# A fused two-pass attention layer, one core: three queues put in another order inside one unit of work

## What is computed

```
q, k, v = xn @ Wq * scale, xn @ Wk, xn @ Wv          # 16 heads of 64
attn    = softmax(causal(q @ k.T))                   # 1024 x 1024 a head
out     = attn @ v
adj     = clip(attn + eye, 0, 1);  deg = adj.sum(-1)
feats   = v
for l in 0, 1:                                       # two graph layers
    h     = feats @ gnn_w[l] + gnn_b[l]
    feats = gelu(adj @ h / deg + feats)
out     = out + feats @ lin_w + lin_b
return layernorm(concat(out) @ Wo)
```

## Time and profile before

| | |
|---|---|
| median of 3 runs | 1946.68 us (1943.61 to 1954.76) |
| the profiled execution's own time | 1947.65 us |
| its span, first to last instruction | 1945.8 us |
| busy in the span: PE, DVE, ACT, POOL | 74%, 60%, 45%, 43% |
| first attention | about 30 to 1044 us |
| busy in it: PE, DVE, ACT, POOL | 850, 547, 555, 522 us |
| granted PE clock in it, share of full speed | 0.96 |
| granted PE clock over the span | 0.874 |
| one whole unit, 312.33 to 372.73 us | 60.40 us, of which PE busy 51.69 |

### The profile page before, as it was taken

The page is one execution under the profiler, slowest core; times in us unless marked ns, Lnnn a source line. Parts: engine busy times, 40 slices in busy tenths (PEclk is TensorE's granted clock), DMA queues, the critical chain, the costliest instruction groups (busy, mean ns, idle before and its releaser), DMA issues. The chain is left out here.

```text
span 1945.8 us, 26818 instructions
## 1 busy us (share of the span) xinstructions
PE 1446.5 (74%) x8265; PEld 935.1 (48%) x8265; DVE 1175.9 (60%) x2921; ACT 881.4 (45%) x1838; POOL 834.7 (43%) x564
## 2 busy tenths in 40 slices
PE   3788888889878888888885877975328575667776
PEld 2555555555555555555544545653325321222466
DVE  4556555565546555565555854467672479999844
ACT  2456555565545555565643622322102175545334
POOL 1455445564444445665551010000005207999535
PEclk9899999999999999999998866887558777989868
DMA  1000000000000000000000000000521212322112
GB/s 54 6 6 1 5 5 5 5 0 5 6 6 1 7 6 5 5 0 5 0 1 13 1 7 6 12 20 0 186 33 37 71 35 84 102 77 92 57 45 84
DMA packets 42464, 53.45 MB, mean 27 GB/s; under 512 B 8529, under 2 KB 29930, under 8 KB 42130
## 3 DMA queue, kind: packets, MB, share of 16 engines
q1 hardware_dynamic: 39634, 46.84, 7.9%
q0 software_dynamic: 2752, 5.65, 1.2%
HBM read 42.82 MB, written 9.26 MB: 27 GB/s over the span
## 5 line engine op out<-in xcount | busy, mean ns | idle before, releaser
L372 POOL TENSOR_TENSOR l0a_A<-l0a_A,l0a_share 128x256 f32<-128x256 f32 (+7 forms) x128 | 269.6, 2107 | 147.3 <-DVE l0a_share L929 147.0
L489 ACT ACTIVATE l0a_A<-l0a_ring,l0a_low 128x512 f32<-128x512 f32 (+3 forms) x384 | 217.6, 577 | 116.1 <-DVE l0a_low L922 74.9
L688 PE MATMUL l0a_tr<-main_ident,l0a_A 128*128 128x128 f32 x1152 | 174.3, 289 | 39.0 <-DVE l0a_E L934 22.7
L934 DVE COPY l0a_E<-l0a_tr 128x512 f32<-128x512 f32 (+1 forms) x160 | 102.0, 638 | 157.8 <-PE l0a_tr L688 157.8
L919 DVE TENSOR_REDUCE l0a_low_part<-l0a_ring 128x2 f32<-128x1024 f32 (+3 forms) x128 | 130.5, 1021 | 97.5 <-PE l0a_ring L669 90.9
L688 PEld LDWEIGHTS l0a_tr<-main_ident,l0a_A 128*128 128x128 f32 x1152 | 136.5, 148 | 79.3 <-issue 57.3
L2857 PE MATMUL mx_ysum<-mx_hst,main_ident 128*128 128x512 f32 x256 | 134.1, 658 | 41.5 <-POOL mx_hst L2976 33.7
L2991 POOL TENSOR_TENSOR mx_dBu<-mx_XI,mx_BB 128x1024 f32<-128x1024 f32 x64 | 139.5, 2207 | 50.0 <-DVE mx_DT L3031 50.0
L378 POOL TENSOR_TENSOR l0a_T<-l0a_VW,l0a_small 128x512 f32<-128x512 f32 x32 | 33.4, 1043 | 277.2 <-DVE l0a_small L952 277.2
L697 PE MATMUL l0a_agg<-l0a_E,l0a_F 128*64 128x512 f32 (+3 forms) x768 | 143.9, 504 | 2.6 <-ACT l0a_U L510 2.6
L697 PE MATMUL l0a_agg<-l0a_E,l0a_VH 128*64 128x512 f32 (+3 forms) x768 | 130.9, 489 | 13.3 <-ACT l0a_E L495 13.3
(11 more groups left out here) (507 smaller groups left out, 3519.6 us busy)
## 6 DMA issues: line engine op xcount, KB each, us to landing
mx_BB<-mx_brows SPq DMA_DIRECT2D x32, 512.0 KB, 3.6
l0a_wp<-in_wqkv SPq DMA_DIRECT2D x16, 192.0 KB
moe_rows<-moe_XR SPq DMA_DIRECT2D x2, 1032.0 KB
moe_Wg<-in_f_wg SPq DMA_DIRECT2D x8, 256.0 KB, 5.7
moe_Wu<-in_f_wu SPq DMA_DIRECT2D x8, 256.0 KB, 5.9
moe_Wd<-in_f_wd SPq DMA_DIRECT2D x8, 256.0 KB, 6.0
moe_Y<-rt_zeros SPq DMA_DIRECT2D x2, 1024.0 KB, 10.9
e_back<-moe_Y SPq DMA_DIRECT2D x8, 256.0 KB, 5.1
```

What stands on the lines that cost most here:

```text
L372: pool.tensor_tensor(a, a, spread(share[:, it, :], [P, 2, w]), ALU.mult).then_inc(shared, 1)
L489: act.activation(A[:, it % 3, h, c0:c0 + n], pair(k % 2)[:, h, 0:n], ACT.Exp, bias=low[:, it, h:h + 1], accum_out=s).then_inc(exp_done, 1)
L688: mm = pe.transpose(tr[n % 2][:, at:at + P], A[:, it % 3, h, t * P:(t + 1) * P], ident[:, :])
L934: dve.tensor_copy(dst, src).then_inc(turned_dve, 1)
```

## The change

Everything keeps its instructions and their shapes; they stand in another order, and the weights of one unit that is never computed are loaded and split too.

- **Weights.** `weights_hi(u + 1)` and `weights_lo(u + 1)` now stand inside the scores of body g, one body earlier than before: ACT does it ahead of the last two exponentials' pieces, POOL between `shares(u, 6)` and `out2(g, 0)`. SP loads one more set.
- **Late score pieces.** On PE `mix` moves from behind pieces 3 and 5 to behind pieces 7 and 9, the tiles of `second(g, 1)` are spread further, and both `product2` come behind pieces 10 and 11. ACT, DVE and POOL move the steps that hang on them. POOL's `out_sum` stand ahead of `shares(u, 5)` and `shares(u, 6)`, and `out2(g, 0)` ahead of `shares(u, 7)`.
- **Turn 11** moves from the end of the scores behind `attend(g, 0)`. Its copy on DVE now stands behind `own_share(g, 0)` and `own_factors(g, 0)`, which come from behind the copies of turns 13 to 19 to the head of the body.
- **Body.** `values(u, 0)` stands ahead of `attend(g, 1)`; `set_own(g, 1)` behind the first two maxima of the scores.

The diff, without that one function of PE:

```diff
--- before.py
+++ after.py
@@ -343,8 +343,7 @@
                 with sp.Fori(0, PAIRS - 1) as i:
                     g = i + b * PAIRS if b else i
                     weights(bass.ds((i + 1) * P, P), g + 1)
-                if b < NB - 1:
-                    weights(slice(0, P), PAIRS * (b + 1))
+                weights(slice(0, P), PAIRS * (b + 1))
 
         @block.gpsimd
         def _(pool):
@@ -412,13 +411,13 @@
                         weights_lo(0)
                 keep_vb(0, 0)
                 keep_vb(0, 1)
-                for it in range(ST):
+                for it in range(ST - 1):
                     shares(0, it)
+                weights_lo(1)
+                shares(0, ST - 1)
 
             def body(g, prev, nb):
                 u, more, third = g + 1, nb is not None, prev is not None
-                if more:
-                    weights_lo(u)
                 own_part(g, 0)
                 own_part(g, 1)
                 if more:
@@ -432,19 +431,20 @@
                     shares(u, 3)
                     keep_vb(u, 0)
                     keep_vb(u, 1)
+                    shares(u, 4)
                 if third:
                     out_sum(g, prev, 0)
                 if more:
-                    shares(u, 4)
+                    shares(u, 5)
                 if third:
                     out_sum(g, prev, 1)
+                if more:
+                    shares(u, 6)
+                    weights_lo(u + 1)
                 out2(g, 0)
                 if more:
-                    shares(u, 5)
+                    shares(u, 7)
                 out2(g, 1)
-                if more:
-                    shares(u, 6)
-                    shares(u, 7)
 
             def tail(n, at):
                 out_sum(n, at, 0)
@@ -537,29 +537,29 @@
                 if more:
                     exps(u, 2)
                     exps(u, 3)
-                if third:
-                    keep_gl(g, 0)
-                if more:
                     turn_out(u, 0)
                     exps(u, 4)
                     exps(u, 5)
-                if third:
-                    keep_gl(g, 1)
-                if more:
                     turn_out(u, 2)
                     exps(u, 6)
                     exps(u, 7)
+                if third:
+                    keep_gl(g, 0)
+                if more:
                     turn_out(u, 4)
-                if second:
-                    keep_u2(g, 1)
-                if more:
                     turn_out(u, 6)
                     exps(u, 8)
                     exps(u, 9)
+                if second:
+                    keep_u2(g, 1)
+                if third:
+                    keep_gl(g, 1)
+                if more:
                     turn_out(u, 8)
-                    turn_out(u, 10)
+                    weights_hi(u + 1)
                     exps(u, 10)
                     exps(u, 11)
+                    turn_out(u, 10)
                 if second:
                     keep_ua(g)
 
@@ -580,7 +580,6 @@
             def body(g, prev, nb):
                 u, more, third = g + 1, nb is not None, prev is not None
                 if more:
-                    weights_hi(u)
                     keep_comp(u)
                 keep_ut(g, 0)
                 if more:
@@ -600,9 +599,10 @@
                     keep_v(u, 0)
                 if third:
                     keep_ft(g, 0)
+                if more:
+                    keep_v(u, 1)
+                if third:
                     keep_ft(g, 1)
-                if more:
-                    keep_v(u, 1)
                 gelu1(g, 1)
                 scores(u if more else None, g, prev)
 
@@ -776,39 +776,44 @@
...
@@ -827,6 +832,7 @@
                     pe.wait_ge(turned_act, g * NK + 6)
                     composite(u)
                 attend(g, 0)
+                turn(g, 11)
                 if more:
                     pe.wait_ge(exp_done, g * NEXP + (NEXP - 2))
                     if not third:
@@ -838,15 +844,16 @@
                 if more:
                     pe.wait_ge(exp_done, (g + 1) * NEXP)
                     project(u, ring[1], 1, nb, k_ready)
-                turn(g, 14, 15)
+                turn(g, 14, 15, 16, 17)
                 product1(g, 0)
-                turn(g, 16, 17, 18, 19)
+                turn(g, 18, 19)
+                if more:
+                    values(u, nb, 0)
                 attend(g, 1)
-                if more:
-                    values(u, nb, 0)
+                if third:
+                    turn_f(g, 0)
                 product1(g, 1)
                 if third:
-                    turn_f(g, 0)
                     turn_f(g, 1)
                 if more:
                     values(u, nb, 1)
@@ -865,7 +872,7 @@
                 more = n < NB * PAIRS
                 pe.wait_ge(exp_done, (n + 1 if more else n) * NEXP)
                 pe.wait_ge(turned_act, n * NK + 6 if more else n * NK)
-                pe.wait_ge(turned_dve, n * NK + 6 if more else n * NK)
+                pe.wait_ge(turned_dve, n * NK + 5 if more else n * NK)
                 pe.wait_ge(ot_kept, n * 2 - 2)
                 out_tiles(0, PAIRS - 1, 0, 1)
                 turn_f(n, 0)
@@ -977,6 +984,9 @@
                 more, second = u is not None, g is not None
                 if more:
                     row_low(u, 0, 1)
+                if second:
+                    set_own(g, 1)
+                if more:
                     row_share(u, 0)
                     row_low(u, 2)
                     row_share(u, 1)
@@ -991,22 +1001,20 @@
                     row_share(u, 4)
                     row_low(u, 7)
                     turn_out(u, 5)
-                if second:
-                    out2(g, 0)
-                if more:
                     row_low(u, 8)
                     row_share(u, 5)
                     row_low(u, 9)
                     turn_out(u, 7)
-                if second:
-                    out2(g, 1)
-                if more:
                     row_low(u, 10)
                     row_share(u, 6)
                     row_low(u, 11)
+                if second:
+                    out2(g, 0)
+                if more:
                     turn_out(u, 9)
-                    turn_out(u, 11)
                     row_share(u, 7)
+                if second:
+                    out2(g, 1)
 
             def first():
                 composite_lo(0)
@@ -1018,6 +1026,9 @@
                 u, more = g + 1, nb is not None
                 if more:
                     composite_lo(u)
+                own_share(g, 0)
+                own_factors(g, 0)
+                turn_out(g, 11)
                 turn_out(g, 13)
                 if more:
                     keep_q_lo(u)
@@ -1026,14 +1037,11 @@
                     keep_k_lo(u)
                 turn_out(g, 17)
                 turn_out(g, 19)
-                own_share(g, 0)
-                own_factors(g, 0)
+                own_share(g, 1)
+                own_factors(g, 1)
                 out1(g, 0)
                 set_own(g, 0)
-                own_share(g, 1)
-                own_factors(g, 1)
                 out1(g, 1)
-                set_own(g, 1)
                 scores(u if more else None, g)
 
             def tail(n, prev):
```

More of the change, by code:

```diff
@@ L778, in scores @@
                     score(u, 2, 3)
+                    turn(u, 0, 1, prev=prev)
+                if two:
+                    second(g, 1, 0, 1)
+                if more:
+                    score(u, 4, 5)
+                    turn(u, 2, 3)
+                if two:
+                    second(g, 1, 2, 3, 4)
+                if more:
+                    score(u, 6)
+                if two:
+                    second(g, 1, 5)
+                if more:
+                    score(u, 7)
                 if three:
@@ L782, in scores @@
                 if more:
-                    turn(u, 0, 1, prev=prev)
+                    turn(u, 4, 5)
                 if two:
-                    second(g, 1, 0)
+                    second(g, 1, 6)
                 if more:
-                    score(u, 4, 5)
+                    score(u, 8, 9)
+                if two:
+                    second(g, 1, 7)
+                if more:
+                    turn(u, 6)
                 if three:
@@ L790, in scores @@
                 if more:
-                    turn(u, 2, 3)
+                    turn(u, 7, 8)
+                    score(u, 10, 11)
                 if two:
-                    second(g, 1, 1, 2, 3)
-                if more:
-                    score(u, 6)
-                if two:
-                    second(g, 1, 4)
-                if more:
-                    score(u, 7)
-                    turn(u, 4, 5)
-                if two:
-                    second(g, 1, 5, 6, 7)
                     product2(g, prev, 0)
                 if more:
-                    score(u, 8, 9)
-                    turn(u, 6, 7, 8)
+                    turn(u, 9, 10)
```

(3 more changed lines are left out.)

24 lines of the change are left out of this document (12 added, 12 removed).

## The result

| | before | after |
|---|---|---|
| median of 11 runs each | 1946.68 us (1940.12 to 1954.76) | 1959.4 us (1955.79 to 1964.05) |
| ratio, 95% interval | | 1.0063 (1.0046 to 1.0080) |
| profiled execution, its span | 1947.65, 1945.8 us | 1956.93, 1955.2 us |
| busy in the span: PE, DVE, ACT, POOL | 74%, 60%, 45%, 43% | 74%, 65%, 45%, 43% |
| first instruction of the layer behind the attention | 1063.3 us | 1074.2 us |

The changed kernel is 0.6% slower. I had forecast 1967 us, 1.0% slower, for the reason that the records now show: a wait taken out at one place came back at another. The size was too large: attention ends 10.9 us later where I had forecast 20.5.

What follows compares the result with a forecast made beforehand. PE's queue with its waits was taken to set the 60.40 us unit. Seven units at +1.1 and six at +1.8 (+18.5), batch starts 0 and -3, last unit +5: +20.5 on 1947.65, so 1968, median 1967 us; range 1938 to 1990.

Steps and rivals of the forecast that it cites:

- piece 0 to 4: Score pieces 0 to 4 on PE: 10.20 us instead of 9.76, with turn 1 waiting about 1.0 for POOL.
- T to composite: From score piece 10's start (T) to the composite on PE: 7.30 us instead of 5.22, waiting for ACT's copy of turn 10.
- composite to Q: From the composite to the Q projection on PE: 3.27 us instead of 6.52, with no pause for POOL's weights.
- Q to piece 0, with the clock: Q projection to the next unit's score piece 0 on PE: 24.2 us at full clock plus 1.3 for slowed clock; before 21.93.
- Q to turn 13: Q's start to turn 13's start on PE: 6.2 us, as POOL's scaling holds DVE's diagonal ahead of turn 11's copy.
- no hold: Rival: DVE and POOL don't hold each other; turn 13 starts 1.9 behind Q, unit 55.6, 1888 us; chance 0.13.
- early diagonal: Rival: DVE's diagonal is issued before POOL's long scaling; 2 to 3 us a unit less, about 1930 us; chance 0.07.
- Turn 13 to piece 0: PE from turn 13 to the next unit's score piece 0: 17.5 us plus the turn's 0.49, at full clock.
- The clock: Behind PE's 4.3 us pause before turn 13, slowed work costs 1.3 us a unit, bounds 0 and 2.4.
- The batches' ends: A batch's first body has no `out_sum`: about 0 in batch one, -3 in batch two, where POOL has nothing left.
- The last unit: No weights to wait for; it pays the late turn 13 in full, some 8 us, less gains and swallowed waits: +5.
- the clock rival: Rival: the clock stays up or its loss is hidden; 59.9 a unit, +4 in all, 1950 us; chance 0.17.

Runs made afterwards that it cites:

- experiment 1: The changed kernel with DVE's diagonal and its factors moved behind the copies of turns 11 and 13: 1953.19 us, ratio 0.9890 to the kernel before.
- experiment 2: The changed kernel with each diagonal instruction replaced by a one-input row sum (TENSOR_REDUCE), so other factors: 1952.62 us, ratio 0.9874 to the kernel before.
- experiment 7: The kernel before with only the first half's diagonal and factors moved to the head of DVE's body: 1975.94 us, ratio 0.9992.
- experiment 8: The changed kernel with one-input row sums for the diagonal and the copies of turns 11 and 13 ahead of the factors: 1918.24 us, ratio 0.9695.
- experiment 3: The kernel before with only the weights split one unit further ahead: 1903.07 us, ratio 0.9631.
- experiment 5: The kernel before with weights a unit ahead, turn 11 behind the first aggregation and the next values ahead of the second: 1888.74 us, ratio 0.9545.

## Why the prediction was right, and where its size was off

The steps by place, in the unit 310.21 to 370.48:

| stretch on PE | predicted | measured |
|---|---|---|
| piece 0 to 4 | 10.20 | 10.24 |
| 4 to 6 | 4.79 | 4.78 |
| 6 to 8 | 4.93 | 5.06 |
| 8 to 10 | 5.19 | 5.19 |
| T to composite | 7.30 | 7.29 |
| composite to Q | 3.27 | 3.13 |
| Q to piece 0, with the clock | 25.5 | 24.58 |
| unit | 61.2 | 60.27 |

- *Score pieces, composite, Q*: all as worked out. Composite waits 1.56 for ACT's copy of turn 10, and turn 1 waits 0.98 for POOL.
- *Q to turn 13*: predicted 6.2, measured 6.06. The step on which the forecast rested, that a SCALAR_TENSOR_TENSOR beside POOL's scaling waits for its end, was taken from two single rows and was right; experiments 1, 2, 7 and 8 show it as the cause. The rival "no hold" gave 55.6 a unit, and with the hold taken away it is 54.87. The rival "early diagonal" is refuted in an instructive way: the first instruction did come before the long scaling (311.52 against 311.84), yet only one passes between two POOL instructions, and the second was held.
- *Turn 13 to piece 0*: predicted 17.5 + 0.49 at full clock. The unit that starts at 370.48 shows it, 397.00 - 379.70 = 17.30. Here 0.7 was too much, and 0.4 of it is a misreading: the old unit's 17.64, which I took for work at full clock, begins at a granted clock of 0.50. There the projection at 323.14 took 1.89 to the turn behind it; here it takes 381.57 - 380.08 = 1.49. The rows, before and after:

```profile
325.03 0.82 PE L688 MATMUL l0a_tr<-main_ident,l0a_A 128*128 128x128 f32 x6
```

```profile
380.08 0.49 PE L640 MATMUL l0a_ring<-l0a_XH,l0a_WH 128*128 128x512 f32 x1
...
381.57 0.82 PE L688 MATMUL l0a_tr<-main_ident,l0a_A 128*128 128x128 f32 x6
```

  The rest is a turn of 0.38 instead of 0.49 and some 0.2 in the work behind it; the waits there, 0.95 and 0.11, are about the 1.0 that was put in.
- *The clock*: 1.3 was taken for each unit. Where the slow stretch follows turn 13 (granted clock 0.58 from 319.40 to 322.40) it costs 337.92 - 319.40 - 17.30 = 1.22, so the size is right there (1.1 to 2.0 in the seven regular units where it does). But it doesn't follow it in each. In the unit from 370.48 it lies in `attend(g, 0)` (granted clock 0.53 from 370.89 to 374.50), 4.07 instead of 2.37, ahead of the wait, and the wait is then 2.32 instead of 3.99: turn 13 starts 9.22 behind the composite, as in the other unit (9.19). Here the slow work lay in front of a wait that DVE's copy ends, and cost nothing. That unit took 59.09. Of the six regular units in the first batch, three have the slow stretch there (`attend` 3.99, 3.80, 4.07; units of 58.2, 59.8 and 59.1, the 59.8 with a second slow stretch behind turn 13) and three behind turn 13 (60.4, 60.3, 60.1); of the five in the second batch one has it in `attend` (59.9, again with a second one).
- *The batches' ends*: predicted -3 for the first body of the second batch, since POOL has nothing left to hold DVE with. It hasn't: the eight diagonal instructions take 0.29 each. But they run only at 578.01, behind 4.7 us of the layer norm's work in DVE's queue (573.11 to 577.77), and turn 13's bank waits for the copies behind both. PE's rows, then DVE's:

```profile
578.19 1.09 PE L688 MATMUL l0a_tr<-main_ident,l0a_A 128*128 128x128 f32 x4 [5.18 <-issue]
581.20 1.09 PE L688 MATMUL l0a_tr<-main_ident,l0a_A 128*128 128x128 f32 x4 [1.92 <-DVE l0a_E L941]
```

```profile
576.54 1.23 DVE L1069 TENSOR_TENSOR main_x<-main_x,l0a_U 128x1024 f32<-128x1024 f32 x1
...
578.01 0.28 DVE L948 SCALAR_TENSOR_TENSOR l0a_scrap<-l0a_E,main_ident 128x128 f32<-128x128 f32 x1
```

- *The last unit*: predicted +5 and a late turn 13 of some 8 us; turns 13 and on wait 7.25 at 1003.19.

The sum in the two profiled traces, where attention ends 10.9 later, against my +20.5:

| part | predicted | measured |
|---|---|---|
| up to the first regular unit | 0 | -0.6 |
| six regular units of the first batch | +6.6 | -2.6 |
| the unit across the batches, first body of the second | -1.9 | +1.6 |
| five regular units of the second batch | +9.0 | +4.8 |
| last regular unit and the end | +6.8 | +7.7 |
| sum | +20.5 | +10.9 |

The first four lines are worked out from the composite's starts: before, 132.4, 493.1, 633.5 and 930.5, after:

```profile
L631 PE MATMUL l0a_tr<-l0a_gnn_lin,l0a_wvT x14: 275/372/482, 131.8 to 489.9; 128*128 128x128 f32 x14
L631 PE MATMUL l0a_tr<-l0a_gnn_lin,l0a_wvT x12: 275/372/577, 631.9 to 933.7; 128*128 128x128 f32 x12
```

A row's last start is that of a unit's second composite instruction, 0.1 to 0.3 behind the first, so the table is good to some 0.2. The last line is what remains to the next layer's first instruction. The term that was mis-sized is the regular unit, 61.2 against (489.9 - 131.8) / 6 = 59.7 and (933.7 - 631.9) / 5 = 60.4: 0.7 from turn 13 to piece 0, and the clock's 1.2 in the units in which it is covered. The batch's end was wrong in sign and hid 3.5 of that error. The sign of the whole was in part luck: the eleven regular units, forecast at +15.6 together, came to +2.2, and most of the +10.9 lies in the last unit and the end, a term forecast by rough reckoning. The regular units average 59.7 and 60.4 against 61.2 in the forecast and 59.9 in the clock rival, which was right in that the loss is hidden in some of them, and wrong in that it isn't in most; the measured 1959.4 us lies about midway between the two. What no run here separates is why the slow stretch lies in `attend` in one unit and behind turn 13 in the next.

## What to carry to other kernels

Before a DVE instruction is moved up in its queue, look at what POOL runs at its new place, how long that runs, and what stands behind the DVE instruction: in experiment 7 the hold cost nothing (0.9992), and with two copies that PE waits for queued behind it, it cost 5.4 us a unit. When a wait is removed, go on along the same engine's queue by hand with the durations of the trace, since the next late thing can be as large; here it could be placed to 0.2 us. And try the parts of a change alone: three of the parts together are worth 4.5%, while the whole of it loses 0.6%.

## What the runs showed of the hardware that was not expected

- **A narrow instruction with one input is held too.** In experiment 2 a TENSOR_SCALAR f32, SBUF to SBUF, of only 8 columns took up to 3249 ns beside POOL (170 at best), while the TENSOR_REDUCE of 128 columns of SBUF took at most 288 there:

```profile
L956 DVE TENSOR_SCALAR l0a_small<-l0a_own x32: 170/173/3249, 80.8 to 979.1; 128x8 f32<-128x8 f32 x32
```

- **Other kinds are held as well.** `set_own`, a COPY_PREDICATED with the inputs `main_ident` and `l0a_one`, took 2.52 us for four instead of 1.46 beside POOL's L380, and the addition of `out1`, a TENSOR_TENSOR of two SBUF tiles, 1.02 instead of 0.69 beside L377 (330.83, POOL's 330.26 to 331.30).
- **The two engines take turns.** In the unit from 310.21, with both queues full, one DVE instruction passes between two of POOL's (0.52, 3.67, 1.34, then 0.28).
- **Held time is shown as duration.** No idle time and no wait is recorded on DVE; only its busy time rises (33.22 to 39.27 us a unit, and to 36.36 in experiment 7, where the hold costs nothing), and only the maximum in a line's min/median/max tells of it.
- **In these traces the longest pause doesn't tell whether the clock falls.** Behind the pause of 3.73 us it was 0.50. The unit of experiment 1 from 610.84 to 668.84 has no pause of PE over 1.6 us and a granted clock of 0.97. The kernel before kept 1.00 from 872.21 to 930.28, with this row of PE's in it:

```profile
878.69 0.50 PE L640 MATMUL l0a_ring<-l0a_XH,l0a_WH 128*128 128x512 f32 x1 [3.69 <-POOL l0a_WL L360]
```

In the units of experiments 3, 5 and 8 read above it was 1.00 too.
